# Attention on one core: stretches of column-tile products hold four weighed steps and two totals where they held two and one, with up to eight buffers for the exponentials

## The reference, cut to what matters

```
x = x + 0.5 * ffn(layernorm(x))        # FP4 weights, 512 -> 2 x 1408 -> 512
x = x + attention(layernorm(x))
x = x + 0.5 * ffn(layernorm(x))
# attention: x is (2, 2048, 512); 16 heads of 32
scores = einsum('bhqd,bhkd->bhqk', Q, K) / sqrt(32)
scores = where(causal, scores, -inf)
A = softmax(scores, axis=-1)
AV = einsum('bhqk,bhkd->bhqd', A, V)
return AV @ Wo + bo
```

## Time and profile before

| | |
|---|---|
| median of 3 runs | 2569.63 us |
| the profiled execution, its own time | 2570.1 us |
| its span, first to last instruction | 2568.3 us |
| PE busy | 2478.6 us, 97% of the span |
| DVE / POOL / ACT busy | 1770.7 / 1543.9 / 1465.2 us |
| granted TensorE clock over the span | 0.995 |
| attention of batch 0, of batch 1 (from the first stay to the last) | 769 to 1267 us, 1463 to 1962 us |

### The profile page before, as it was taken

The page is one execution under the profiler, slowest core; times in us unless marked ns, Lnnn a source line. Parts: engine busy times, 40 slices in busy tenths (PEclk is TensorE's granted clock), DMA queues, the critical chain, the costliest instruction groups (busy, mean ns, idle before and its releaser), DMA issues.

```text
span 2568.3 us, 39616 instructions
## 1 busy us (share of the span) xinstructions
PE 2478.6 (97%) x14559; PEld 1100.9 (43%) x14559; DVE 1770.7 (69%) x3016; ACT 1465.2 (57%) x2829; POOL 1543.9 (60%) x1604
## 2 busy tenths in 40 slices
PE   5899999999999999999999999999999999999998
PEld 3444444444443434333344434444333444444443
DVE  7866666667659594948486695858575866666665
ACT  6666666665225656566622256565655466666665
POOL 3467666764316767676442267676774467766775
PEclk9999999999999999999999999999999999999999
DMA  2012211121122020200231312020004301111101
GB/s 67 17 47 78 91 41 50 50 99 66 33 60 61 12 46 22 52 6 2 88 128 34 81 41 52 7 52 22 3 4 149 123 17 50 50 50 50 50 33 50
DMA packets 78017, 130.58 MB, mean 51 GB/s; under 512 B 19551, under 2 KB 24698, under 8 KB 77694
## 3 DMA queue, kind: packets, MB, share of 16 engines
q1 hardware_dynamic: 77822, 128.05, 16.2%
HBM read 68.23 MB, written 31.46 MB: 39 GB/s over the span
## 4 chain that ended last, share of the span: by engine, by line
PE 77%; POOL 6%; DVE 6%; ACT 4%; issue 2%; SPq 1%; DMA 0%; POOLq 0%; DVEq 0%; ACTq 0%
PE pp L97 59%; PE ps L97 17%; POOL sb L106 5%; ACT sb L103 4%; DVE sb L112 2%; DVE sb L118 1%; SPq L139 1%; PE ps L100 1%; POOL sb L109 1%; DVE sb L106 1%; PE pp L100 0%; DVE sb L115 0%; DMA sb<-sb 0%; DVE sb L109 0%; DVE sb L124 0%
## 5 line engine op out<-in xcount | busy, mean ns | idle before, releaser
L97 PE MATMUL pp<-sb,sb 128*128 128x512 f16 (+8 forms) x11230 | 2068.8, 420 | 32.6 <-DVE sb L112 14.4
L106 POOL TENSOR_TENSOR sb<-sb,sb 128x512 f32<-128x512 f32 (+7 forms) x1353 | 1490.9, 1127 | 993.2 <-PE pp L97 330.4
L97 PEld LDWEIGHTS pp<-sb,sb 128*128 128x128 f16 (+3 forms) x11230 | 799.8, 102 | 1068.5 <-issue 214.5
L97 PE MATMUL ps<-sb,sb 128*128 128x512 f16 (+8 forms) x2786 | 723.1, 348 | 26.8 <-DVE sb L112 13.6
L103 ACT ACTIVATE sb<-pp 128x512 f32<-128x512 f32 (+6 forms) x1035 | 521.2, 560 | 331.2 <-PE pp L97 317.3
L118 DVE TENSOR_REDUCE sb<-pp 128x1 f32<-128x512 f32 (+3 forms) x704 | 441.0, 667 | 150.2 <-PE pp L97 150.0
L103 ACT ACTIVATE sb<-sb 128x512 f16<-128x512 f32 (+4 forms) x513 | 326.0, 650 | 366.0 <-DVE sb L112 306.4
L112 DVE SCALAR_TENSOR_TENSOR sb<-pp,sb,sb 128x512 f32<-128x512 f32 x447 | 324.6, 746 | 151.5 <-PE pp L97 136.6
L112 DVE SCALAR_TENSOR_TENSOR sb<-ps,sb,sb 128x512 f32<-128x512 f32 x437 | 318.1, 747 | 154.7 <-PE ps L97 128.7
L97 PEld LDWEIGHTS ps<-sb,sb 128*128 128x128 f16 (+3 forms) x2786 | 251.3, 97 | 339.9 <-DVE sb L118 36.0
L103 ACT ACTIVATE sb<-ps 128x512 f32<-128x512 f32 (+5 forms) x473 | 262.7, 566 | 155.3 <-PE ps L97 123.2
(11 more groups left out here) (29 smaller groups left out, 373.3 us busy)
## 6 DMA issues: line engine op xcount, KB each, us to landing
sb<-sb SPq DMA_DIRECT2D x144, 128.0 KB, 2.4
sb<-L_attn_X SPq DMA_DIRECT2D x64, 256.0 KB, 3.4
sb<-xa SPq DMA_DIRECT2D x64, 256.0 KB, 4.2
sb<-xc SPq DMA_DIRECT2D x64, 256.0 KB, 3.4
xa<-sb SPq DMA_DIRECT2D x32, 256.0 KB, 2.0
xc<-sb SPq DMA_DIRECT2D x32, 256.0 KB, 4.4
out<-sb SPq DMA_DIRECT2D x32, 256.0 KB, 2.0
sb<-sb SPq DMA_DIRECT2D x48, 96.0 KB, 2.2
```

What stands on the lines that cost most here:

```text
L97: return self.e.matmul(*a, **k) if self.e else self
L106: return self.e.tensor_tensor(*a, **k) if self.e else self
```

## The change

- **Longer stays.** From step 16 on a stay is weigh m, weigh m + 1, total m - 3, total m - 1, weigh m + 2, weigh m + 3 (`'01ST23'`); before step 16 it is weigh, weigh, total. A stay may start when all four of its steps are scored. There are 44 stays in a batch. The last two totals follow the last stay.
- **Lead of the scores.** Scores may lead by 9 or 10 products beyond the next stay's steps (4 before); the weights of the planner's choice are other numbers.
- **E buffers.** `place` is gone. The planner picks for each step the buffer that its clocks free first, among 4 (n < 16), 6 (n < 48), 7 (n < 88), 8 (n < 120) and 6 again; four of the ten lie where `ks`, the keys of a head group, lay, and ScalarE waits for the copies of those keys before their first use. The buffer of an odd step is free after its add, head by head, and not only after the total.
- **`Wo`.** Its load is issued after the stay that starts with step 120 and waits for total 119; before, after the scores of step (2, 1, 0). `wo_split` follows the scores of step (3, 1, 4), before (2, 3, 0).
- **`late`** is a set of odd steps; it holds 147 to 159, the same steps as before.

```diff
-        self.E = [p.at([128, 4, 512], F32, x) for x in [o + 8192 * i for i in range(NE)] + [QS0 + 98304, QS0 + 106496]]
+        self.E = [p.at([128, 4, 512], F32, x) for x in [o + 8192 * i for i in range(NE)] +
+                  [QS0 + 98304, QS0 + 106496, C0, C0 + 8192, C0 + 16384, C0 + 24576]]
...
+        def released(k):
+            if k is None:
+                return 0.0
+            if k % 2:
+                return max(added[k], weigh_end[k]) if k in added else None
+            return sum_end.get(k + 1)
+
+        def pick(n):
+            most = range(NE) if n < 16 else (0, 1, 2, 3, 6, 7, 8, 9)[:6 + (n >= 48) + (n >= 88)] if n < 120 else range(6)
+            known = [(released(hold[i]), i) for i in most if released(hold[i]) is not None]
+            return min(known) if known else None
...
-            first = 4 * n + j < 4 * m + 8
+            seq_of = "01T" if m < 16 else '01ST23'
+            long = 2 if m < 16 else 4
+            first = 4 * n + j < 4 * m + 4 * long
-            if ready and 4 * n + j < 4 * m + 8 + (4 if wide else 4):
+            if ready and 4 * n + j < 4 * m + 4 * long + (9 if wide else 10):
...
-            if n >= m + 2 and (m == 0 or m - 1 in added):
+            if n >= m + long and (m == 0 or m - 1 in added):
-                for x in '0T1':
+                for x in seq_of:
...
-                seq = [("total", m - 1) if x == "T" else ("weigh", m + int(x)) for x in '0T1']
-                m += 2
+                seq = [("total", m - 1 if x == "T" else m - 3) if x in "ST" else ("weigh", m + int(x)) for x in seq_of
+                       if x != "S" or m != 16]
+                if m == 120:
+                    seq.append(("wo", None))
+                m += long
...
-                      if steps[n] == (2, 1, 0):
-                          out.append(("wo",))
-                      if steps[n] == (2, 3, 0):
+                      if steps[n] == (3, 1, 4):
                           parts.extend(("wo_split", c) for c in range(KC))
...
-            if m is None:
+            if m is None and place < NE:
+                e.wait_ge(*p.qkv.proj_done.at((b, "values", 3, 3)))
+            elif m is None and place < NE + 2:
                 e.wait_ge(*t.exp_done.at((b, t.last_step(2), 3)))
-            elif m >= 0:
-                e.wait_ge(*t.sum_done.at((b, m + 1 - m % 2)))
+            elif m is None:
+                group = max(1, place - NE - 2)
+                for head in range(4):
+                    e.wait_ge(*t.stacked[group % 2][head].at((b, group)))
+            elif m % 2 == 0:
+                e.wait_ge(*t.sum_done.at((b, m + 1)))
             else:
-                e.wait_ge(*p.qkv.proj_done.at((b, "values", 3, 3)))
+                e.wait_ge(*t.av_done.at((b, m)))
+                e.wait_ge(*(t.late_added.at((b, m, j // 2)) if m in t.late[b] else t.e_added.at((b, m, j))))
...
+            e.wait_ge(*t.sum_done.at((b, 119)))
             e.dma_start(p.out.wraw[:, :, :], p.a["L0_attn_Wo"].rearrange("(c p) n -> p c n", p=128)).then_inc(
```

More of the change, by code:

```diff
@@ L1324, in __init__ @@
         self.banks = [Banks() for _ in range(B)]
-        self.late = [0] * B
+        self.late = [set() for _ in range(B)]
+        self.slots = {}
         self.late_added = p.sign("a_late_added")
         self.plan = [list(self.order(b)) for b in range(B)]
[L1329 to L1335, removed]
     def offset(self, n):
@@ L1456, in order @@
                     work = 0
-                need = sum(4 * (512 - self.offset(k)) / 2.4 + 20 for k in (m, m + 1, *((m - 2,) if m else ())))
+                need = sum(4 * (512 - self.offset(m + int(x) if x.isdigit() else m - (2 if x == "T" else 4))) / 2.4 + 20
+                           for x in seq_of if x.isdigit() or m and (x == "T" or m != 16))
                 idle = clock - pe - 100.000000 - need
-                cand.append((pe + idle + 2500.000000 - 1.000000 * min(max(dve - pe, 0), 2000), "stay", 0))
+                cand.append((pe + idle + 1500.000000 - 0.485000 * min(max(dve - pe, 0), 2000), "stay", 0))
             at, what, i = min(cand, key=lambda x: x[0])
@@ L1474, in order @@
                   pe = at + c / 2.4 + 3 + (57 if kt >= 4 * qt else 0)
-                  place, old = self.place(n)
-                  free = sum_end.get(old + 1 - old % 2, 0.0) if old is not None and old >= 0 else 0.0
+                  if j == 0:
+                      gone, slot = pick(n)
+                      self.slots[n] = slot, hold[slot]
+                      hold[slot] = n
+                  free = gone
                   act = max(act, pe + 235, free) + 0.833 * c + 52
@@ L1515, in order @@
                   if ev == ("rows", 3, 3):
[L1516 removed]
+                      late = scored[0] + 4
               elif what == "combine":
@@ L1521, in order @@
                   out.append(ev)
+              elif what == "wo":
+                  out.append(("wo",))
               elif what == "weigh":
@@ L1529, in order @@
                   if n % 2:
+                      work, start = 4 * c, max(weigh_end[n - 1], exped[n, 3])
+                      if late and n >= late or max(dve, start) + 1.04 * work + 1000000000.000000 < max(pool, start) + 2.117 * work:
+                          self.late[b].add(n)
                       for h in range(4):
                           start = max(weigh_end[n - 1], exped[n, h])
-                          if self.late[b] and n >= self.late[b]:
+                          if n in self.late[b]:
                               dve = max(dve, start) + 1.04 * c + 32
@@ L1549, in order @@
                       inverted = max(dve, sum_end[n]) + 745
-        self.sum_up(out, parts, N - 1)
+        for k in range(N - 4 + 1, N, 2):
+            self.sum_up(out, parts, k)
         yield from out
@@ L1752, in att_dve @@
             n = at[0]
-            if n % 2 and n >= t.late[b]:
+            if n in t.late[b]:
                 add_steps(e, p, b, n, t.late_added)
@@ L1799, in att_pool @@
             n = at[0]
-            if n % 2 and n < t.late[b]:
+            if n % 2 and n not in t.late[b]:
                 add_steps(e, p, b, n, t.e_added, 1)
```

31 lines of the change are left out of this document (17 added, 14 removed).

## The result

The changed kernel took **2604.53 us** (2602.97 to 2605.31, 4 runs) against 2569.95 for the kernel before on the same chip: a ratio of 1.0132, 95% interval 1.0115 to 1.0150. I had forecast 2566.2, within 2542 to 2588. It is slower by 34.6 us and outside the range.

What follows compares the result with a forecast made beforehand. Attention was taken as TensorE's products plus stay switches and about 45 us of waiting a batch. Terms -9.4 - 12.0 + 13.5 + 14.1 - 7.9 = -1.7 a batch, -3.4 in all, gave 2566.2 us, range 2542 to 2588.

Steps and rivals of the forecast that it cites:

- 36 stays less: Attention stays fall from 80 to 44 a batch, each costing 0.26 us beyond its products: -9.4 us a batch.
- Waits inside stays: TensorE's waits for ScalarE and GpSimd inside stays nearly vanish, 1.3 us left: -12.0 us a batch.
- Gaps of scores alone: Seven gaps of 16 scores wait for ScalarE to free banks, 14.3 us in place of 0.8: +13.5 a batch.
- Bank waits in mixed gaps: In 36 gaps with scores and maxima, waits for banks are 27.4 us, before 13.3: +14.1 a batch.
- the rule: A gap between stays lasts the longest of its products, its exponentials or its reductions, less the last six units, plus latencies.
- The rest: Gap waiting that the rule does not give, 17.4 us a batch, falls to 9.5 with fewer gaps: -7.9.
- Rival C: Mixed gaps slower, ScalarE and VectorE near their limits holding each other's banks: 0.3 us more a gap, +22, 2588; chance 0.16.
- Rival B: Bank waits of mixed gaps grow less: half of the 14.1 absent gives 2552, all of it 2538; chance 0.28.
- Rival D: Granted clock falls in the new gaps of scores alone: +14 to +24 us, 2580 to 2590; chance 0.06.
- E: A buffer's release is late and ScalarE's queue stands: one wait of 5 us in each batch, 2576; chance 0.06.

Runs made afterwards that it cites:

- kernel 1: The changed kernel with short stays (weigh, weigh, total) throughout, 79 of them, all else kept: 2582.39 us, 1.0043 of the kernel before.
- kernel 9: The changed kernel with short stays and the planner's old weights, its lead, E buffers and place of `Wo` kept: 2572.73 us, 1.0008 of the kernel before.
- kernels 7 and 8: Kernel before with the change's free choice of E buffers: 2568.10 us; the same plus VectorE making sums in score-only runs: 2552.07 us.
- kernels 4 to 6: The changed kernel with row-maximum reductions over half their columns: 2588.90 us; exponentials over half: 2559.70 us; both at half: 2510.02 us.
- kernel 6: The changed kernel with both exponentials and row-maximum reductions over half their columns, work left out: 2510.02 us, 0.9766 of the kernel before.
- kernel 8: Kernel before with free choice of E buffers and VectorE making sums in score-only runs where it ends earlier than GpSimd: 2552.07 us, 0.9933.

## Why the prediction was wrong

Per batch, by its own steps (forecast, then batch 0 of the trace):

- *36 stays less*, -9.4: held. The cost of going in and out of a stay is as in rows 3; here too the stay starts 0.32 after the last product's start and the next full product comes 0.97 after the last load of the stay.
- *Waits inside stays*, -12.0: 17.4 less 3.8, without the constant 0.05 of the 36 stays, is -11.8. Right.
- *Gaps of scores alone*, +13.5: they take 15.2 over their products, before 1.5. Right (the 0.2 more are in the last item).
- *Bank waits in mixed gaps*, +14.1: the rule gives this and a single gap can follow it (before step 96: 8.83 against 8.60). It is a floor, no more.
- ***The rest*, -7.9: this step failed.** What the gaps take beyond the rule was 18.0 us before (17.4 in the prediction) and is 27.9 now: +9.9, an error of 17.8 a batch and 35.6 in all, of a miss of 38.3. I let the unexplained time shrink with the number of gaps. It does not depend on that number: with 79 short stays and everything else of the change it is 28.6 (kernel 1), with 44 long ones 27.9. And it grew with the other parts of the change, which I had put at nothing: 27.7 in kernel 9, which has the old weights but the change's lead, buffers and place of `Wo`, against 19.8 and 20.0 in kernels 7 and 8, which have lead, weights and `Wo` of before. In the change it stands outside the gaps with splits at 0.50 a gap (20.3 us over 41), before at 0.18 (13.7 over 77), and in the two with splits at 7.5 against 4.3.

The sum is then -9.4 - 11.8 + 13.5 + 14.1 + 9.9 = +16.3, and the attention of batch 0 grew by 16.3.

What is in it: the rule adds up each reader's work over a whole gap and takes the larger sum, as if units of both kinds stood evenly. In the gap before step 36 they stand as 16 scores and nine maxima, and the sums of 5.90 hide a part that waits for ScalarE and one that waits for VectorE. An estimate of mine replays the planned order unit by unit through the six banks, with the times that the prediction took from rows 3, 4 and 6 and without the splits, the DMAs and the waits for E buffers. It gives 2.2 us over the products in that gap (measured 2.4, rule 0.7), and for the batch 5 us over the rule in the kernel before, 11 in the change and 13 in kernel 1. So the order of the units, which the change's weights and lead set, accounts for part of the growth, with short stays as with long ones. It gives only 7 of the 27.7 in kernel 9, so it is not all of it; which of lead, buffers and place of `Wo` makes the remainder was not separated, and no kernel had the units evenly mixed.

What is shown: that 22 us of the loss come with the length of the stays (kernel 1), and that for this part the rule's bank terms hold; that both readers together hold TensorE in the gaps (kernels 4 to 6); and that the rest is as large with short stays (kernels 1 and 9). What stays open is why the other parts of the change raise the rest.

Rival C had the direction and the place, the mixed gaps, and its two readers are real there (before step 96 only both at half give 0.79 us). That they price the rest of the long gaps is not shown, since the rest is as large with short ones. Its 0.3 us a gap over my forecast gave 2588; the trace has 0.5 (27.9 less the 9.5 that I took, over 36 gaps). I gave it 0.16, and my forecast had only the fewer gaps on its side. Rival B was wrong: the mixed gaps take 23.8 us more over their products (30.6 to 54.4), where the rule says 14.1. Rival D was wrong in its place: in a score-only period the granted clock is 1.00 (below), and in batch 0 it fell at the splits alone, for 6.82 us.
```profile
1257.65:1268.80 11.15, 10.35 (x69) 2.97 (x71) 4.72 (x4) 8.00 (x18) 0.58 (x1) 1.00 0.00 0
```
E has 2.6 us of ScalarE waiting for GpSimd in the batch, no single wait of 5.

The Trainium skill (TensorEngine Tiling (Array Packing), Performance Considerations, PSUM Bottleneck) says that reading PSUM can become the bound where tiling makes TensorE's part short. The trace agrees: kernel 6 shows how much hangs on it here, 94.5 us of 2604.5. The page says nothing on how long a tiled run may be.

## What to carry to other kernels

While a run of products leaves the shared banks alone, their readers drain them and then stand idle; lengthening the run to save a switch of 0.26 us is worth it only if the readers have slack behind it. A sum of work over a gap is a floor, missed by 1.7 us here in a gap where the units of each kind stood together. And a remainder that no term explains must not be scaled with the number of gaps on trust: here it was 28 us with 44 stays and with 79, and only a kernel with that number changed and nothing else could show it. When halving one reader gives little, halve both before calling it no bound: the waits pass from one to the other. And when a wait has two causes in series (here E buffers and GpSimd's sums), removing either shows next to nothing, so try them together before dropping both.

## What was not expected of the hardware

The granted clock stayed at 0.50 for a second stretch of 3.40 us in which TensorE was busy for all 3.40 (1194.80 to 1198.20, above), so a thin stretch behind it is paid for in the dense work that follows. In kernel 8 VectorE's sum of a pair of steps takes 2.36 us, where GpSimd's took 4.96 in the kernel before, and VectorE starts it 1.1 us into the stay:
```profile
882.47 2.36 DVE L106 TENSOR_TENSOR sb<-sb,sb 128x1024 f32<-128x1024 f32 x2 [2.24 <-PE pp L97]
```
```profile
880.28 4.96 POOL L106 TENSOR_TENSOR sb<-sb,sb 128x512 f32<-128x512 f32 x4 [0.52 <-PE pp L97]
```
